# Attention stage: reciprocal sums in two parts spread by one product each, and the output product by branch

## The reference

```python
def _mha(x, Wqkv, bqkv, Wo, bo):
    qkv = x @ Wqkv.T + bqkv
    q, k, v = jnp.split(qkv, 3, axis=-1)
    ...
    scores = jnp.einsum('...qhd,...khd->...hqk', q, k) * scale
    a = jax.nn.softmax(scores, axis=-1)
    o = jnp.einsum('...hqk,...khd->...qhd', a, v).reshape(*lead, S, D)
    return o @ Wo.T + bo
...
res = outs[0] * w[0]
for i in range(1, n):
    res = res + w[i] * outs[i]
```

## Time and profile before

| | |
|---|---|
| Median of 3 runs | 3874.93 us (3874.57 to 3878.07) |
| Profiled execution | 3871.27 us |
| Its span, first to last instruction | 3869.5 us |
| Attention stage, first scores to last eviction | 1073.65 to 2124.03 us |
| Mean granted TensorE clock over the span | 0.98 |

### The profile page before, as it was taken

How to read it: one execution, slowest core, us unless ns; L and a number is a source line. 1 busy time by engine, 2 the same in 40 slices (tenths; PEclk the granted TensorE clock), 3 DMA queues, 4 the chain that set the end, 5 groups by cost and what they waited for, 6 DMA issues and landing times. The chain is left out here.

```text
span 3869.5 us, 79181 instructions
## 1 busy us (share of the span) xinstructions
PE 3675.1 (95%) x27464; PEld 3183.8 (82%) x27464; DVE 3248.2 (84%) x7738; ACT 2736.3 (71%) x7878; POOL 2451.5 (63%) x2324
## 2 busy tenths in 40 slices
PE   6999999999789999999998699999999979999989
PEld 5888888888678888888886588888888868898878
DVE  7999999999678888888875799999999958756577
ACT  6777777777389999999996677777777648532166
POOL 7788887887365555555541777887788737411365
PEclk8999999999899999999999899999999989999999
DMA  4655655665400000000000466655566542421442
GB/s 117 123 120 119 122 118 117 120 125 113 102 13 13 24 13 24 13 24 13 24 7 18 119 121 120 122 119 119 117 120 125 114 100 88 127 90 57 149 132 93
DMA packets 189486, 339.98 MB, mean 88 GB/s; under 512 B 14720, under 2 KB 138016, under 8 KB 189088
## 3 DMA queue, kind: packets, MB, share of 16 engines
q0 software_dynamic: 54432, 198.21, 27.0%
q1 hardware_dynamic: 134656, 136.71, 11.2%
HBM read 80.06 MB, written 56.62 MB: 35 GB/s over the span
## 5 line engine op out<-in xcount | busy, mean ns | idle before, releaser
L302 POOL TENSOR_TENSOR f_grid<-f_ex 128x1024 f32<-128x1024 f32 x512 | 1161.8, 2307 | 0.3 <-DVE f_q L730 0.3
L1551 ACT ACTIVATE a_ex<-a_p_s,a_mneg 128x128 f32<-128x128 f32 x2048 | 726.0, 406 | 90.7 <-DVE a_mneg L1609 90.7
L721 DVE SCALAR_TENSOR_TENSOR f_p_u<-f_grid,f_te,f_p_dot 128x1024 f32<-128x1024 f32 x512 | 655.1, 1280 | 43.1 <-PE f_p_dot L106 42.3
L730 DVE SCALAR_TENSOR_TENSOR f_q<-f_p_u,f_rz,f_grid 128x1024 f32<-128x1024 f32 x512 | 655.0, 1279 | 10.9 <-PE f_p_wT L447 6.3
L312 POOL DMA_DIRECT2D f_q<-f_q x378 | 380.2, 1006 | 377.1 <-DMA f_q<-f_q 266.5
L1551 ACT ACTIVATION_READ_ACCUMULATOR a_ex<-a_p_s,a_mneg 128x1 f32 x2048 | 503.5, 246 | 0.0
L460 PE MATMUL f_p_y<-f_wdn,f_hs 128*128 128x256 f32 x2048 | 487.6, 381 | 1.3
L465 PE MATMUL f_p_y<-f_eup,f_wT 128*128 128x256 f32 x2048 | 473.1, 379 | 0.0
L465 PEld LDWEIGHTS f_p_y<-f_eup,f_wT 128*128 128x128 f32 x2048 | 380.1, 190 | 46.5
L460 PEld LDWEIGHTS f_p_y<-f_wdn,f_hs 128*128 128x128 f32 x2048 | 370.9, 191 | 44.0 <-issue 3.4
L1609 DVE TENSOR_REDUCE a_mneg<-a_p_s 128x4 f32<-128x512 f32 x512 | 335.5, 676 | 7.1 <-PE a_p_s L1404 7.1
(11 more groups left out here) (645 smaller groups left out, 11089.5 us busy)
## 6 DMA issues: line engine op xcount, KB each, us to landing
f_q<-f_q POOLq DMA_DIRECT2D x378, 512.0 KB, 4.8
x_f<-f_yt SPq DMA_DIRECT2D x64, 256.0 KB, 2.2
f_xt<-x SPq DMA_DIRECT2D x32, 256.0 KB, 3.3
a_xt<-x_f SPq DMA_DIRECT2D x16, 512.0 KB, 3.9
x_a<-a_yt SPq DMA_DIRECT2D x16, 512.0 KB, 2.9
f_xt<-x_a SPq DMA_DIRECT2D x32, 256.0 KB, 3.3
c_xt<-x_f SPq DMA_DIRECT2D x16, 512.0 KB, 4.7
x_c<-c_yt SPq DMA_DIRECT2D x16, 512.0 KB, 3.1
```

Of the source, the lines that this page charges most:

```text
L302: g_grid.mark(pool.tensor_tensor(grid[v][:, hd, :].rearrange("p (i j) -> p i j", i=XROWS), sx[:, hd, :].unsqueeze(2).to_broadcast([P, XROW ...
L721: d_mask.mark(dve.scalar_tensor_tensor(out=p_u[:], in0=grid[v][:, hd, :], scalar=te[:, v, hd, TOP - 1:TOP], in1=p_dot[:], op0=ALU.is_ge, o ...
L730: d_mul.mark(dve.scalar_tensor_tensor(out=q[v][:, hd, :], in0=p_u[:], scalar=rz[:, v, hd:hd + 1], in1=grid[v][:, hd, :], op0=ALU.mult, op1 ...
L1551: last = act.activation(ex[t.step % 2][:, i, n, :], p_s[i][:, n, :], ACT.Exp, bias=mneg[:, i, n:n + 1], accum_out=z[t.step % 2][:, i, n:n ...
```

## The change

1. `rz` is split in two: `rest` on VectorE writes the reciprocals rounded to fp32r (`upper`) and the difference (`lower`) side by side into `rz_hl` (64 columns, 16 of each 32 used). One transpose takes both into 64 rows of `p_t`, `turned_rz` copies 64 rows to `rzT` in fp32r, and `spread`, loaded twice below each other and copied to fp32r once, has 64 rows. Each half of `repeat` is then one fp32r product.
2. `put_out` makes a piece of 128 tokens by 256 columns for one branch: two products of 256 columns. VectorE adds branch 0 to `xb`, and branch 1 to what it wrote to `yt` for branch 0.
3. `p_y` is now the whole second half of `p_ox`, and `p_h` moves to the second quarter of `p_t`. VectorE's `evict` does `turn_h` first and waits for the output product after that; TensorE's wait for `d_hT` moves from `attend` to the transposes of quad 3.
4. The last row's output goes through `put_last`, one segment of 128 tokens in each score bank, both branches added up there, without waits between them. Segments 0 and 1 are made ahead of the end of the last unit, since no part of the last unit is in them.

```diff
-        spread = m.sbuf("spread", DC, P)
+        spread = m.sbuf("spread", DC, P, dt=F32R)
...
-        p_y, p_h = p_ox[:, 1, 0:P], p_ox[:, 1, P:2 * P]
+        p_last = [p_s[v][:, 0:2, :].rearrange("p n k -> p (n k)") for v in range(SEGS)]
+        p_y, p_h = p_ox[:, 1, :], p_t[:, 1, :]
...
-                    if i == QUAD - 1 and (t - 1).exists():
-                        d_rzT.wait(pe, t - 1)
+                    if i == QUAD - 1:
+                        if (t - 1).exists():
+                            d_rzT.wait(pe, t - 1)
+                        next_row, part = part_of(t)
+                        if next_row.exists(last=rows):
+                            d_hT.wait(pe, next_row, str(part))
...
-                        last = pe.matmul(p_rep[:, c, :], spread[0:SLOT, c, :], rzT[0:SLOT, :], start=True, stop=True)
+                        last = pe.matmul(p_rep[:, c, :], spread[0:2 * SLOT, c, :], rzT[0:2 * SLOT, :], start=True, stop=True)
...
                 def put_out(r, b):
-                    v, k = b // 2, b % 2
+                    v, br = b // BR, b % BR
+                    for c in range(DC):
+                        last = pe.matmul(p_y, oT[r.step % 2][br][:, c, v * P:(v + 1) * P], wo[:, br, c, :],
+                                         start=c == 0, stop=c == DC - 1)
+                    t_y.mark(last, str(b))
+
+                def put_last(v):
                     for br in range(BR):
                         for c in range(DC):
-                            last = pe.matmul(p_y, oT[r.step % 2][br][:, c, v * P:(v + 1) * P], wo[:, br, c, k * P:(k + 1) * P],
+                            last = pe.matmul(p_last[v], oT[last_row.step % 2][br][:, c, v * P:(v + 1) * P], wo[:, br, c, :],
                                              start=br == c == 0, stop=(br, c) == (BR - 1, DC - 1))
-                    t_y.mark(last, str(b))
+                        t_y.mark(last, str(BR * v + br))
...
                 turn_ex(last_unit, 3)
+                d_ex.wait(pe, last_unit, "2")
+                d_o.wait(pe, last_unit - 1)
+                put_last(0)
                 turn_rz(last_unit)
                 attend(last_unit)
                 repeat(last_unit)
+                put_last(1)
                 d_o.wait(pe, last_unit)
-                for b in range(UR):
-                    if b:
-                        d_y.wait(pe, last_row, str(b - 1))
-                    put_out(last_row, b)
+                put_last(2)
+                put_last(3)
...
+                def rest(t):
+                    d_rz.wait(dve, t, "whole")
+                    upper = rz_hl[:, 0:MH]
+                    d_rz.mark(dve.tensor_copy(upper.bitcast(F32R), rz[:]), "upper")
+                    d_rz.wait(dve, t, "upper")
+                    d_rz.mark(dve.tensor_tensor(rz_hl[:, SLOT:SLOT + MH], rz[:], upper, ALU.subtract), "lower")
...
                     if next_row.exists(last=rows):
-                        t_hT.wait(dve, next_row, str(part))
+                        turn_h(next_row, part)
                     if (r - 1).exists():
                         t_y.wait(dve, r - 1, str(u))
                     if (t - 1).exists():
                         divide(t - 1)
-                    if next_row.exists(last=rows):
-                        turn_h(next_row, part)
```

More of the change, by code:

```diff
@@ L1191, in dilated_attention @@
         z = [m.sbuf(f"z{k}", QUAD, QUAD) for k in range(2)]
-        rz = m.sbuf("rz", SLOT)
-        rzT = m.sbuf("rzT", P)
+        rz, rz_hl = m.sbuf("rz", MH), m.sbuf("rz_hl", 2 * SLOT)
+        rzT = m.sbuf("rzT", P, dt=F32R)
         ex = [m.sbuf(f"ex{k}", QUAD, QUAD, P) for k in range(2)]
@@ L1223, in dilated_attention @@
         t_s, d_max, a_ex, t_ex, d_ex = (m.track(k, *quads) for k in ("t_s", "d_max", "a_ex", "t_ex", "d_ex"))
-        d_rz, t_rz, d_rzT = m.track("d_rz"), m.track("t_rz"), m.track("d_rzT")
+        d_rz, t_rz, d_rzT = m.track("d_rz", "whole", "upper", "lower"), m.track("t_rz"), m.track("d_rzT")
         t_av, t_rep, a_rep, d_o = (m.track(k) for k in ("t_av", "t_rep", "a_rep", "d_o"))
@@ L1236, in evicted @@
             u, r = ur_of(t), row_of(t)
-            next_row, part = part_of(t)
-            if next_row.exists(last=rows):
-                d_hT.wait(e, next_row, str(part))
             if (r - 1).exists():
@@ L1274, in _ @@
                 load(first_row + 1)
-                sp.dma_start(spread[0:SLOT], w["spread"]).then_inc(s_w, 16)
+                for k in range(2):
+                    sp.dma_start(rep[k * SLOT:(k + 1) * SLOT], w["spread"]).then_inc(s_w, 16)
                 sp.dma_start(bo[:].rearrange("p r d -> p (r d)"),
@@ L1420, in turn_rz @@
                     d_ex.wait(pe, t, "3")
-                    t_rz.mark(pe.transpose(p_t[0:SLOT, 0, :], rz[:], ident[:]))
+                    t_rz.mark(pe.transpose(p_t[0:2 * SLOT, 0, :], rz_hl[:], ident[:]))
                 def attend(t):
@@ L1475, in _ @@
                     project(first_unit + SEGS, c)
-                pe.wait_ge(s_w, 16 * 3)
+                pe.wait_ge(s_w, 16 * 4)
                 pe.wait_ge(s_b, 1)
@@ L1593, in _ @@
                 dve.memset(half[:], -0.5).then_inc(s_c, 1)
-                dve.memset(rz[:], 0.0)
+                dve.memset(rz_hl[:], 0.0)
                 for br in range(BR):
@@ L1620, in inverse @@
                         t_rz.wait(dve, t - 1)
-                    d_rz.mark(dve.reciprocal(rz[:, 0:MH], z[t.step % 2][:].rearrange("p i n -> p (i n)")))
+                    d_rz.mark(dve.reciprocal(rz[:], z[t.step % 2][:].rearrange("p i n -> p (i n)")), "whole")
+                def rest(t):
[4 more added lines that the diff above has]
+                    d_rz.mark(dve.tensor_tensor(rz_hl[:, SLOT:SLOT + MH], rz[:], upper, ALU.subtract), "lower")
                 def turned_rz(t):
@@ L1626, in turned_rz @@
                         t_rep.wait(dve, t - 1)
-                    d_rzT.mark(dve.tensor_copy(rzT[0:SLOT, :], p_t[0:SLOT, 0, :]))
+                    d_rzT.mark(dve.tensor_copy(rzT[0:2 * SLOT, :], p_t[0:2 * SLOT, 0, :]))
                 def divide(t):
@@ L1646, in put_out, with put_last @@
                             slot_wait(dve, s_st, r - 2)
-                    d_y.mark(dve.scalar_tensor_tensor(out=yt[r.step % 2][:, v, cols], in0=p_y, scalar=BRANCH_WEIGHT,
-                                                      in1=xb[r.step % 2][:, v, cols], op0=ALU.mult, op1=ALU.add), str(b))
+                    if br:
+                        d_y.wait(dve, r, str(b - 1))
+                    rest = (yt if br else xb)[r.step % 2][:, v, :]
+                    d_y.mark(dve.scalar_tensor_tensor(out=yt[r.step % 2][:, v, :], in0=p_y, scalar=BRANCH_WEIGHT,
+                                                      in1=rest, op0=ALU.mult, op1=ALU.add), str(b))
+                def put_last(v):
+                    r = last_row
+                    t_y.wait(dve, r, str(BR * v + BR - 1))
+                    if v == 0:
+                        g_xb.wait(dve, r)
+                        slot_wait(dve, s_st, r - 2)
+                    dve.scalar_tensor_tensor(out=yt[r.step % 2][:, v, :], in0=p_last[v], scalar=BRANCH_WEIGHT,
+                                             in1=xb[r.step % 2][:, v, :], op0=ALU.mult, op1=ALU.add).then_inc(d_y.sem, BR)
                 def evict(t):
@@ L1721, in _ @@
                     d_hT.mark(dve.tensor_tensor(lo, p_s[3][:, b - SEGS, :], hi.bitcast(F32), ALU.subtract), str(b))
-                dve.wait_ge(s_w, 16 * 3)
+                dve.wait_ge(s_w, 16 * 4)
+                dve.tensor_copy(spread[0:2 * SLOT], rep[0:2 * SLOT])
                 dve.tensor_tensor(bos[:, 0, :], bo[:, 0, :], bo[:, 1, :], ALU.add).then_inc(s_b, 1)
@@ L1739, in step @@
                         turned(t - 1, 3)
+                        rest(t - 1)
                     if u == 1 and (r + 2).exists(last=rows):
@@ L1757, in _ @@
                 turned(last_unit, 3)
+                rest(last_unit)
+                put_last(0)
                 turned_rz(last_unit)
                 divide(last_unit)
-                for b in range(UR):
-                    put_out(last_row, b)
+                for v in range(1, SEGS):
+                    put_last(v)
 UNSEEN = 1e-9
```

2 lines of the change are left out of this document (1 added, 1 removed).

## The result

The changed kernel takes 3893.16 us (median of 5 runs, 3888.93 to 3899.06) against 3874.79 us of the kernel before on the same chip: 1.0056 of it, with a 95% interval of 1.0039 to 1.0073. It is slower by 15 to 28 us, where 9.5 us less were forecast, and it lies outside the range.

What follows compares the result with a forecast made beforehand. The prediction took a ring of waits through four engines in the attention units as the bound. Its terms, -4.7 + 3.6 - 0.2 - 8.2 = -9.5 us, took 3874.9 to 3865.4 us, range 3857 to 3874.

Steps and rivals of the forecast that it cites:

- The steady part: Attention units before the stage's end: -4.7 us without statistics, +3.6 us with them, -0.2 us in the last row.
- Middle units: Attention units between first and last rows, without statistics: 8.015 us each, forecast at 7.96 us.
- VectorE's added work: Per unit 0.44 us more: 0.14 us for the wider output step, 0.30 us for two 16-column steps; hidden in most units.
- The upper bound: The two 16-column steps on VectorE: at most 0.53 us, as two dependent steps as long as the 128-column subtraction.
- Rival 3: VectorE becomes the bound and ScalarE stalls in every unit: +38 us, less 8, 3905 us; chance 0.06.
- 0.9 us of cover: Time in a unit between quad 2's maximum and ScalarE's need of it, hiding VectorE's added steps up to 0.9 us.
- Units with statistics: The 14 units u = 1, rows 0 to 13, where VectorE hardly pauses: 0.26 us more each, +3.6 us.
- the ring: The chain of waits through four engines that sets a unit's time, with TensorE having at least 0.21 us to spare.
- The order: turn_h ahead of the division on VectorE: 0.02 us a unit, with the output product by branch 0.05 us.
- The spread: Two fp32r records for four float32 ones free some 0.22 us of TensorE a unit; gain on the ring zero.
- The end of the stage: Last row's output through four score banks without waits between products: -8.2 us, bounds -9.0 and -5.0.
- rival 2: TensorE's last output groups run at 1.2 GHz, losing 3 to 4 us of the 8.2: 3869 us; chance 0.11.

Runs made afterwards that it cites:

- experiment 5: The changed kernel with GpSimd's key difference and four masked key copies cut to 8 of 512 columns from the second row on: 3854.16 us in one execution.
- experiment 1: The changed kernel without the split of the reciprocals (one float32 transpose of 32 columns, float32 spread): 3859.18 us, 0.9970 of the kernel before.
- Experiment 9: The changed kernel without the split of the reciprocals and with turn_h back behind the division: 3875.47 us in one execution.
- experiment 4: The kernel before with only the last row's output moved to the score banks (put_last): 3858.42 us, 0.9967 of the kernel before.
- experiment 10: The kernel of experiment 1 (changed kernel without the split) measured again, beside that of experiment 4 on one chip: 3860.55 us, 0.9967 of the kernel before.
- experiment 11: The kernel of experiment 4 (kernel before with the new end alone) measured again on another chip: 3862.76 us, 0.9975 of the kernel before.
- experiment 3: The kernel before with the split of the reciprocals alone (rest, transpose of 64 columns, fp32r spread): 3901.25 us, 1.0078 of the kernel before.
- experiment 7: The changed kernel without the 16-column subtraction, the lower part left zero: 3861.34 us in one execution.
- experiment 8: The changed kernel with the rounded upper part written by a second reciprocal from the sums instead of the cast: 3869.39 us, 0.9992 of the kernel before.

## Why the prediction was wrong

- **The steady part: wrong in one term.** Middle units came to 7.95 to 8.02 us (forecast 7.96), but u = 1 to 9.86 (8.27) and u = 4, 5 to 8.40 and 8.36 (7.96). The step that failed is the price of the two 16-column steps in *VectorE's added work*: 0.30 us, and at most 0.53 us. I bounded them by small steps of the earlier trace rows and by a subtraction of 128 columns. None of these is of the same kind: they read PSUM, or are reductions and aggregations. Small was taken as the property that matters, where kind and place of the operands were. Measured: 0.33 us when GpSimd is idle, up to 1.98 us when it isn't. The term held only the steps' own work and no wait for another engine.
- **The upper bound was not one.** "As long as a wider step" bounds the work of a step, not the wait for something shared. The profile of the kernel before held a row that says so, and that I did not read. GpSimd's products run 1064.70 to 1065.73 and on to 1066.92:

```profile
1065.14 0.87 DVE L1723 TENSOR_TENSOR a_bos<-a_bo 128x256 f32<-128x256 f32 x1
```

  A step of 128 x 256 with one operand in PSUM takes 0.43 us; this one, with both in SBUF, takes 0.87: 0.59 us to the end of a GpSimd product, and 0.28 us after it.
- **Rival 3 was the right end by half a mechanism.** It said VectorE would become the bound and asked for 0.5 us a step; I gave it 0.06 because no small step was that long. It priced the loss in every unit (+38 us, less 8 for the end); it comes in three of eight, 31 us. Of its 0.9 us of cover u = 0 is a sign: 0.95 us for the two steps cost that unit nothing.
- **Units with statistics: right.** With undisturbed steps u = 1 takes 8.22 us (experiment 5) against 8.27. That VectorE has no slack there, so that the ring pays for what it gets, was right. But the wider output step alone costs nothing (experiment 1).
- **The order: right in size, not in its parts.** 0.02 to 0.03 us a unit for 0.05. The sum also left 12 of the 128 units out (94 + 14 + 8 = 116), which at 0.05 us would be 0.6 us. Experiment 9 shows that the parts I priced one by one depend on each other.
- **The spread: right.** Two fp32r records take 0.44 us for four of 0.71 (they start 0.16 us apart, not 0.11), and in the ring it comes to nothing: middle units take 7.99 us with float32 (experiment 1) and 7.98 with fp32r. The gain ends in the wait for ScalarE, which was 0.21 us and was forecast at about 0.40:

```profile
1829.78 0.42 PEld L1418 LDWEIGHTS a_p_s<-a_ident,a_ex 128*128 128x128 f32 x4 [0.43 <-ACT a_ex L1562]
```

  Only the end of the stage keeps it: from the division of the last unit but one to the last eviction the kernels with the new end take 10.20 us with the float32 spread (experiments 1, 4, 9, 10, 11) and 9.93 us with the changed kernel's. There was next to no gain to set against the two steps.
- **The end of the stage: right in size, with the clock's help.** 9.93 us against 9.8 forecast, 8.07 us saved for 8.2. The last 24 records took 5.45 us (5.2), the first eight 1.97 us (1.73). The forecast set new products at full clock against 13.66 us in which the old ones had partly run at half, so 1.4 us of its gain were a bet that the clock would stay up; rival 2 is that bet lost. It stayed up in this stretch in all eleven profiles with the new end and fell in both with the old one (granted clock 0.62 from 2110.37 to 2114.83 in the kernel before, 0.76 from 2139 to 2146 in experiment 3). TensorE had stood idle for 0.92 us just ahead of the first of the old pieces; that the missing waits keep the clock up is likely, but no run here separates the two.

## What to carry to other kernels

Before a step is added to VectorE, read two things beside its size: where its operands lie, and what GpSimd does at that moment in the timeline. A cast of a tile in SBUF, or a step with two operands in SBUF, took six times its length there; the same work from PSUM, or as a reciprocal, did not. A stall in three units of eight is thinned out in a group's mean, so price a new step by its longest instance, in the unit that has no slack, and ask first whether what it buys ends in a wait.

## What the runs showed of the hardware

- A 16-column cast and a 16-column subtraction in SBUF take 0.16 and 0.17 us alone, and in the changed kernel up to 1.02 and 0.97 us beside GpSimd instructions of 1.04 to 1.28 us (1.09 us at most in experiments 3, 7 and 8); a reciprocal of 16 columns takes 0.23 to 0.25 us in all 1,664 instances, of which 1,392 ran beside a GpSimd instruction.
- Beside GpSimd's TENSOR_SCALAR (u = 3) the subtraction takes 0.17 to 0.18 us and the cast 0.33 to 0.34 us in all of the rows 1 to 13 of the changed kernel, while the GpSimd instruction takes 1.23 us: neither waits for its end. Why, no run here shows.
- A waiting cast was passed over by four GpSimd instructions that followed each other without a pause (1.74 us). Shorter instructions on GpSimd helped in u = 4 and 5 and did harm in u = 2: no safe remedy.
